# Two-layer gated block on one core: the argmax counts turned by DMA instead of TensorE, a new opening, pieces of 256, 512, 512, 512

## The reference, cut to what matters

```python
xn = layernorm(x)                                   # rows of 512, no scale or shift
w  = weight * (mask of 32x32 blocks is on)          # 512 x 512
s  = xn @ w.T + bias
inter = xn @ c1_w.T @ c2_w.T                        # rank 16, then 1792 columns
idx = argmax of inter in each of the 56 blocks of 32 columns
h   = relu(xn . w1[idx]);  g = silu(h @ w2t[idx])   # only the 56 chosen rows count
x   = x + s * g
```

## Time and profile before

| | us |
|---|---|
| median of 3 runs | 694.86 (693.66 to 695.56) |
| profiled execution, device time | 693.95 |
| its span, first to last instruction | 692.2 |
| mean granted TensorE clock | 0.993 |

### The profile page before, as it was taken

One profiled execution on the slowest core, in us unless ns is written; L12 is line 12 of the kernel. 1 busy time (PEld: TensorE's weight loads), 2 busy tenths in 40 slices (PEclk: granted clock), 3 DMA queues, 4 the chain that ended last, 5 costly groups with the idle time before them and its releaser, 6 DMA issues.

```text
span 692.2 us, 8636 instructions
## 1 busy us (share of the span) xinstructions
PE 659.1 (95%) x3078; PEld 518.1 (75%) x3078; DVE 457.0 (66%) x715; ACT 214.4 (31%) x379; POOL 231.7 (33%) x185
## 2 busy tenths in 40 slices
PE   2699999999999999999999999989999999999997
PEld 2577777877787777787777777657877877787787
DVE  7877775596665596665597776674856566485543
ACT  3424343312222412222312233443145125313610
POOL 1516455450000540000661226433514242341441
PEclk9899999999999999999999999999999999999999
DMA  8940000040000130000152110040031013002001
GB/s 235 386 166 1 0 1 0 32 152 1 0 1 0 47 136 0 0 0 0 45 207 80 58 62 0 32 153 0 31 110 43 1 45 136 0 30 91 2 16 46
DMA packets 19535, 40.66 MB, mean 59 GB/s; under 512 B 2032, under 2 KB 2416, under 8 KB 18864
## 3 DMA queue, kind: packets, MB, share of 16 engines
q1 hardware_dynamic: 19504, 40.25, 16.8%
HBM read 31.85 MB, written 8.39 MB: 58 GB/s over the span
## 4 chain that ended last, share of the span: by engine, by line
PE 84%; DVE 10%; issue 3%; DMA 1%; ACT 1%; POOL 0%; SPq 0%; DVEq 0%; ACTq 0%
PE bank L404 74%; PE bank L338 2%; PE bank L1141 2%; DVE eq L862 2%; PE bank L1236 2%; DVE seg_top L860 1%; PE bank L1104 1%; PE bank L1122 1%; DVE counts L872 1%; PE bank L1273 1%; DVE h_lo L896 1%; DVE ws_lo L925 1%; DMA x_tile<-in_x 1%; DVE x_tile L378 1%; DVE h L887 0%
## 5 line engine op out<-in xcount | busy, mean ns | idle before, releaser
L404 PE MATMUL bank<-w_hi_t,h_hi 128*128 128x512 f32 x224 | 93.7, 418 | 1.7 <-DVE h_lo L896 1.7
L698 ACT ACTIVATE h_hi<-h 128x512 fp32r<-128x512 f32 x56 | 35.4, 632 | 182.8 <-DVE h L887 182.8
L872 DVE TENSOR_TENSOR_SCAN counts<-restart,eq 128x512 bf16<-128x512 bf16 (+1 forms) x64 | 88.3, 1380 | 2.1
L404 PE MATMUL bank<-xT_hi,w_hi_t 128*128 128x512 f32 x224 | 88.9, 397 | 0.0
L404 PE MATMUL bank<-w_hi_t,h_lo 128*128 128x512 f32 x224 | 88.5, 395 | 0.0
L404 PE MATMUL bank<-w_lo_t,h_hi 128*128 128x512 f32 x224 | 88.5, 395 | 0.0
L404 PE MATMUL bank<-xT_hi,w_lo_t 128*128 128x512 f32 x224 | 88.5, 395 | 0.0
L404 PE MATMUL bank<-xT_lo,w_hi_t 128*128 128x512 f32 x224 | 88.4, 395 | 0.0
L860 DVE TENSOR_REDUCE seg_top<-bank 128x16 f32<-128x512 f32 (+1 forms) x64 | 39.5, 618 | 72.7 <-PE bank L1122 72.7
L384 POOL TENSOR_TENSOR g_tile<-g_tile,s_tile 128x512 f32<-128x512 f32 x31 | 40.6, 1311 | 95.2 <-DVE g_tile L909 56.4
L612 POOL TENSOR_TENSOR prod_lo<-prod,prod_hi 128x512 fp32r<-128x512 f32 x32 | 40.7, 1292 | 74.4 <-ACT prod_hi L736 74.4
(11 more groups left out here) (184 smaller groups left out, 1326.2 us busy)
## 6 DMA issues: line engine op xcount, KB each, us to landing
w_raw<-in_w SPq DMA_DIRECT2D x28, 256.0 KB, 10.1
x_res<-in_x SPq DMA_DIRECT2D x4, 1024.0 KB, 8.2
mid_state<-g_tile SPq DMA_DIRECT2D x16, 256.0 KB, 2.1
x_tile<-mid_state SPq DMA_DIRECT2D x4, 1024.0 KB, 7.6
x_res<-mid_state SPq DMA_DIRECT2D x4, 1024.0 KB, 5.6
out<-g_tile SPq DMA_DIRECT2D x15, 256.0 KB, 2.0
x_tile<-in_x SPq DMA_DIRECT2D x3, 1024.0 KB, 5.4
b_raw<-in_lora_b SPq DMA_DIRECT2D x2, 1024.0 KB, 4.9
```

The lines of the kernel that those rows point to most:

```text
L404: last = nc.tensor.matmul(dst, a, b, start=(start and n == 0), stop=(stop and n == len(mms) - 1))
L698: nc.scalar.activation(h_hi[:, it % 2, :], h[:], ACT.Copy).then_inc(h_hi_done, 1)
L872: nc.vector.tensor_tensor_scan(counts[:, p % 2, tt, 0:PW[p]], restart[:, 0:PW[p]], eq[:, 0:PW[p]], 0.0, ALU.mult, ALU.add).then_inc(sel_co ...
```

## The change

Seven things are changed together, nearly all in layer 0.

1. The counts are turned by DMA. `transpose_counts` is gone from TensorE. After the scan of a selection ScalarE issues one transposing DMA (`turn_counts`) from `counts` to `first`, which now lies in SBUF with two pieces' room; there are 16 for a chunk, of 128x512 or 128x256 bf16. VectorE's mask waits for the landing at the first tile of each piece. `counts` has one piece's room, and a scan waits for the landing of the turn of the piece before.
2. The pieces are 256, 512, 512, 512 wide instead of 512, 512, 512, 256. The selections of piece 0 and of row tiles 0 and 1 of piece 1 stand in the head, the other ten (`NEXT`) at it 0 to 9.
3. Selections use two banks in turn, `sels`; one waits for the equality of the last but one. `h` has two buffers, and relu runs one tile ahead.
4. The rank product of the next chunk moves from the head to the end of the body, between the parts of the last down product, and `t_rest` with it, ahead of the silu.
5. The opening: x comes in four row tiles, each normalized as it lands (`first_rows`); 14 matmuls of constants run first on TensorE; w1 tiles 0 and 1 are loaded ahead, mask and weight behind six others. The mask's block sums come at it 3 of chunk 0, the switch at 4, its products with the weight at 4 and 5, `ws_lo` at 6 and 7, and the s products ahead of up 9 and up 11. The body's first selections of chunk 0 (piece 1) come two per tile at it 0 and 1.
6. Epsilon is added by VectorE, so GpSimd has one instruction for the inverse root. Some constants move between VectorE and GpSimd.
7. In layer 0 GpSimd makes the four products of the gate first and then the four sums.

```diff
-    PW = [min(BANK, INTER - p * BANK) for p in range(PIECES)]
+    PW = [INTER - BANK * (PIECES - 1)] + [BANK] * (PIECES - 1)
+    PO = [sum(PW[:p]) for p in range(PIECES)]
+    AT = [(p, j) for p in range(PIECES) for j in range(PW[p] // P)]
+    NEXT = [(p, tt) for p in range(1, PIECES) for tt in range(S // P)][2:]
...
+        first = span_t.take("first", [P, 2, TT, S], BF16)
+        counts = span_t.take("counts", [P, TT, BANK], BF16)
...
-        h = span_t.take("h", [P, S])
...
+        h = span_t.take("h", [P, 2, S])
...
+        def first_rows(dve):
+
+            for tt in range(TT + 1):
+                if tt < TT:
+                    dve.wait_ge(ld_x if tt == TT - 1 else ld_x_first[tt], 16)
+                    nc.vector.bn_stats(bn[:, tt, :], x_tile[:, tt, :]).then_inc(stats_in, 1)
+                    dve.wait_ge(stats_in, tt + 1)
+                    nc.vector.bn_aggr(mean_var[:, tt, :], bn[:, tt, :]).then_inc(stats, 1)
+                    dve.wait_ge(stats, tt + 1)
+                    nc.vector.tensor_scalar(mean_var[:, tt, 1:2], mean_var[:, tt, 1:2], EPS, None, ALU.add)\
+                        .then_inc(var_eps, 1)
+                if tt:
+                    dve.wait_ge(rstd_done, tt)
+                    rows_scale(tt - 1)
...
-        sel = banks[6]
-        mask_bank = banks[5]
-        first = banks[7][:].bitcast(BF16)[:, 0:S]
+        sels = [banks[6], banks[7]]
+        warm_bank = banks[5]
...
+        WARM = 14
+        WS_AT = (5, 6)
+        MASK_N = TT * NEXT[WS_AT[0] - 1][0] + NEXT[WS_AT[0] - 1][1]
+        S_AT = (9, 11)
...
-            sp.dma_start(mask_nat[:], mask).then_inc(ld_mask, 16)
+            for tt in range(TT):
+                sp.dma_start(x_tile[:, tt, :], x_rows[0][:, tt, :]).then_inc(ld_x if tt == TT - 1 else ld_x_first[tt], 16)
+            sp.dma_start(c1_nat[:], c1_w).then_inc(ld_c1, 16)
+            for it in range(2):
...
+                    sp.dma_start(mask_nat[:], mask).then_inc(ld_mask, 16)
+                    sp.dma_start(ws_raw[:], w_s0).then_inc(ld_ws0, 16)
...
+            def turn_counts(c, p, tt):
+
+                act.wait_ge(sel_count, c * NSEL + p * TT + tt + 1)
+                if p >= 2:
+                    act.wait_ge(h_masked, c * IT + PO[p - 1] // P)
+                elif not (isinstance(c, int) and c == 0):
+                    act.wait_ge(h_masked, c * IT)
+                act.sem_inc(turns, 1)
+                act.dma_start_transpose(first[:, p % 2, 0:PW[p] // P, rows(tt)], counts[:, tt, 0:PW[p]])\
+                    .then_inc(ld_first[tt], 16)
+
             def head(c):
-                t_round(c)
-                for tt in range(TT):
+                for tt in range(2):
                     s_read(c, tt)
+                    turn_counts(c, 0, 2 * tt)
+                    turn_counts(c, 0, 2 * tt + 1)
+                for tt in range(2, TT):
+                    s_read(c, tt)
+                turn_counts(c, 1, 0)
+                turn_counts(c, 1, 1)
+                relu(c, 0)
+
...
+                if it in WS_AT:
+                    for k in range(2):
+                        k += 2 * (it - WS_AT[0])
+                        act.wait_ge(ws0_masked, k + 1)
+                        nc.scalar.activation(ws_hi[:, k, :], ws_raw[:, k, :], ACT.Copy).then_inc(ws_hi_done, 1)
+                if it + 2 in S_AT:
+                    for tt in range(2):
+                        s_read(0, 2 * S_AT.index(it + 2) + tt)
...
+                turned = c * PIECES + p
+                if not (isinstance(turned, int) and turned == 0):
+                    dve.wait_ge(ld_first[tt], turned * 16)
...
-                t_rest(c)
-                for tt in range(TT - 1):
+                for tt in range(TT):
                     select(c, 0, tt)
-
-            def body(c, last):
-                select(c, 0, TT - 1)
+                for tt in range(2):
+                    select(c, 1, tt)
+
+            def body(c, opening, last):
                 for it in range(IT):
-                    if 0 < it < 4 * (PIECES - 1):
-                        select(c, it // 4 + 1, it % 4)
+                    todo = [(1, 2 * it), (1, 2 * it + 1)] if opening and it < 2 else NEXT[it:it + 1]
                     dve.wait_ge(relu_done, c * IT + it + 1)
-                    dve.wait_ge(first_tr, c * IT + it + 1)
-                    nc.vector.scalar_tensor_tensor(h[:], first, 1.0, h[:], ALU.is_equal, ALU.mult).then_inc(h_masked, 1)
+                    p, j = AT[it]
+                    if j == 0:
+                        for tt in range(TT):
+                            dve.wait_ge(ld_first[tt], (c * PIECES + p + 1) * 16)
+                    nc.vector.scalar_tensor_tensor(h[:, it % 2, :], first[:, p % 2, j, :], 1.0, h[:, it % 2, :],
+                                                   ALU.is_equal, ALU.mult).then_inc(h_masked, 1)
+                    if it == IT - 1:
+                        for tt in range(2):
+                            rows_lo(dve, c + 1, tt)
                     if IT - 8 <= it < IT - 4:
                         rows_stats(dve, c + 1, it - (IT - 8))
...
+                    if opening and it == WS_AT[0] - 1:
+                        mask_switch()
+                    if todo:
+                        select_largest(c, *todo[0])
...
+                    if todo:
+                        select_count(c, *todo[0])
+                    if todo[1:]:
...
+                    if opening:
+                        if it == WS_AT[0] - 2:
+                            mask_counts()
+                        if it == WS_AT[0] - 1:
+                            mask_ws(range(0, 2))
+                        if it == WS_AT[0]:
+                            mask_ws(range(2, 4))
+                        if it in (WS_AT[0] + 1, WS_AT[0] + 2):
+                            ws_rest(range(2 * (it - WS_AT[0] - 1), 2 * (it - WS_AT[0] - 1) + 2))
+                for tt in range(2, TT):
                     rows_lo(dve, c + 1, tt)
+                if not last:
+                    t_rest(c + 1)
                 for tt in range(TT):
 
                     dve.wait_ge(tanh_done, c * TT + tt + 1)
...
+            def s_product(c, tt):
+
+                if isinstance(c, int) and c == 0:
+                    pe.wait_ge(ws_split, KD)
+                    pe.wait_ge(relu_done, S_AT[tt // 2] - 1 + tt % 2)
+                elif tt >= 2:
...
+                n = p * TT + tt
+                if n == 0:
                     pe.wait_ge(t_split, c + 1)
-                else:
-                    pe.wait_ge(sel_eq, c * NSEL + p * TT + tt)
-                nc.tensor.matmul(sel[:, 0:PW[p]], t_stack[:, rows(tt)],
...
-            def transpose_counts(c, it):
-
-                pe.wait_ge(sel_count, c * NSEL + (it // 4 + 1) * TT)
-                if it:
-                    pe.wait_ge(h_masked, c * IT + it)
-                for tt in range(TT):
-                    last = nc.tensor.transpose(first[:, rows(tt)], counts[:, it // 4 % 2, tt, rows(it % 4)], ident_bf[:])
-                last.then_inc(first_tr, 1)
...
-                rank_product()
+                select(c, 0, 0)
+                select(c, 0, 1)
                 s_product(c, 0)
+                select(c, 0, 2)
+                select(c, 0, 3)
                 s_product(c, 1)
-                select(c, 0, 0)
+                select(c, 1, 0)
+                select(c, 1, 1)
                 s_product(c, 2)
-                select(c, 0, 1)
                 s_product(c, 3)
-                select(c, 0, 2)
-
-            def body(c, first):
-                if not first:
...
+            def body(c, first, last):
+                for it in range(1, IT):
+                    if first and it in S_AT:
+                        s_product(0, 2 * S_AT.index(it))
+                        s_product(0, 2 * S_AT.index(it) + 1)
+                    if first and it - 1 in S_AT:
+                        pe.wait_ge(s0_read, 2 * S_AT.index(it - 1) + 2)
+                    elif first and it in S_AT:
+                        pe.wait_ge(s0_read, 2 * S_AT.index(it) + 1)
+                    up_product(c, it)
+                    if first:
+                        first_chunk(it)
+                    elif it <= len(NEXT):
+                        select(c, *NEXT[it - 1])
                     if it >= 2:
                         pe.wait_ge(h_split, c * IT + it - 1)
-                        if first and it == 2:
-                            pe.wait_ge(s0_read, TT)
                         down_product(it - 2, range(TT)).then_inc(down_done, 1)
+                        if first and it == 3:
+                            select(0, *NEXT[2])
+                pe.wait_ge(sel_eq, c * NSEL + NSEL)
+                for tt in range(2):
+                    transpose_rows(pe, c + 1, tt)
+                pe.wait_ge(relu_done, c * IT + IT - 1)
+                transpose_rows(pe, c + 1, 2)
                 pe.wait_ge(relu_done, c * IT + IT)
-                transpose_rows(pe, c + 1, 1)
```

(16 more changed lines are left out.)

371 lines of the change are left out of this document (193 added, 178 removed).

## The result

The changed kernel takes 719.84 us (median of 4 runs, 717.33 to 723.27) against 694.26 (4 runs, 692.24 to 695.56): ratio 1.037, 95% interval 1.0329 to 1.041. It is slower, as the largest of the three chances said, but far outside the range of 684 to 707. The profiled execution took 720.03, its span 718.2.

The account below looks back on a forecast made before the run. TensorE was taken to bound the kernel, VectorE the changed opening. Profiled 693.95 + 10.6 (chunk 0) - 5.8 (heads) - 3.5 (chunk 3) = 695.2, forecast 696 as median; range 684 to 707, own range 691 to 702.

Parts of the forecast that it names:

- the largest of the three chances: Whole kernel: slower, chance 0.44, against faster 0.39 and same 0.17.
- Chunk 0, forecast +10.6: Chunk 0 ends at about 139 instead of 128.4, 10.6 us lost; bounds 1.5 and 21 lost.
- Start: Opening: rank product starts at 13.5 instead of 16.41, 2.9 us saved; 1.6 more if the warmed clock is high.
- the fourth rival: Opening: warming does nothing, rank product at 0.43 again, all later by 1.6: 698 us; part of the forecast's range.
- L: Time from a scan's end to the landing of its turned counts: 3 us, bounds 2 and 5.
- The rival of late turns: From L = 4.5 each chunk waits at piece 1, chunk 0 three times; 710.5 us at L = 6.5; chance 0.21.
- VectorE's 54.4: Chunk 0, its 0 to 7: VectorE's own work from mask 0 at 28.4 to the last ws_lo, 54.4 us.
- Waits, forecast 6.0: Chunk 0, VectorE's waits: 3.0 and 1.5 for turns, 0.5 for the switch, 1 for a queued selection; sum 6.0.
- From the first s product to the end, forecast 51: Chunk 0 after ws_lo: 202 matmuls 47.1 us, row transposes 1.8, half clock 2.
- 88.8 rounded down to 88: Chunk 0, last ws_lo: 28.4 + 54.4 + 6.0 = 88.8, taken as 88 since not every scan meets POOL.
- Heads, forecast 1.9 saved: Chunks 1 to 3: period 100.2 instead of 102.1, 1.9 us saved each, 5.8 in all.
- Chunk 3, forecast 5.4 saved: Chunk 3: the period's 1.9 us saved, and 3.5 off its waits of 3.6 and the pauses beside them.

Follow-up runs that it names:

- e7_sels: Changed kernel with GpSimd's rstd earlier, loads held for two turns, TensorE's heads reordered, and chunk 0's selections issued ahead of products: 700.39 us, ratio 1.0125.
- e2_loads: Changed kernel with SyncE waiting for the four turns of piece 0 before the loads from w1 4 on: 719.85 us, ratio 1.0375.
- e5_pace: Changed kernel with SyncE holding loads twice, for the turns of piece 0 and of piece 1, mask and masked weight behind the second: 721.05 us, ratio 1.0411.
- e1_pool: Changed kernel with chunk 1's rstd put ahead of the last w2 rest and four bias sums on GpSimd: 711.26 us, ratio 1.0231.
- e12: Changed kernel with the masked weight at the front of chunk 0, GpSimd's rstd earlier and TensorE's heads reordered: 699.20 us, ratio 1.007.
- e13: Changed kernel with only the masked weight put back to the front of chunk 0: 714.02 us, ratio 1.0291.
- e3_fill: Changed kernel with twelve idle bf16 products filling TensorE's two waits ahead of s product 1 in heads of chunks 1 to 3: 714.02 us, ratio 1.0293.
- e15_all_rounds: e11_all with ScalarE rounding weights ahead of the turn in chunk 0's steps: 694.44 us, ratio 1.0003.
- e9_spread: e7_sels with later weight loads of chunk 0 each waiting for an up product, mask at step 5, next rows at step 7: 696.59 us, ratio 1.0039.
- e11_all: e9_spread with chunk 0's s products at up 10 and 12, and 16 more idle products ahead of the rank product: 690.88 us, ratio 0.9964.

## Why the prediction was wrong

**Chunk 0, forecast +10.6, measured +25.95.** By its own terms:
- Start. The rank product at 14.11 instead of 13.5, and at half clock: it ends 2.2 us later than forecast (17.58, not 15.4). The warming products ended at 7.69, the row transposes followed, and after 3.04 us of idle time the clock had fallen (0.61 from 14 to 18), as the fourth rival said. Luck has a part in it: in e7_sels, with the same opening, the rank product started at 12.58, after 1.96 us, and took 2.10.
- L, forecast 3 and taken as one number. It is 2.3 to 2.4 with no loads ahead and 7.24 behind loads. I had the row for that (10.1 for a load in the opening) and set it aside because the turns use another queue; e2_loads shows that the other queue does not keep them apart. With the start (1.3 of it), mask 0 came at 34.15 instead of 28.4: +5.8. The rival of late turns had such an L and 710.5 us, but for every turn; here it was piece 0 alone, and no run shows what this lateness costs by itself, since e2_loads and e5_pace only moved it. The Trainium skill (DMA: Bandwidth & Descriptors, Anatomy of one DMA) has a fixed cost and a rate, measured for DMAs that GpSimd issues, from which 128 KB would take an estimated 2.3; the trace agrees for ScalarE's turns with no loads ahead of them (2.42), and not for those behind loads.
- VectorE's 54.4. Measured 46 (mask 0 to the last ws_lo, 60.4, less 14.4 of waits): -8.4. I charged each scan 1.54; alone it takes 1.22, and only 1 of these 10 met GpSimd. The ten selections took 26.1 instead of 30.0, and the four products with the switch and the four ws_lo 4.8 instead of 8.0.
- Waits, forecast 6.0, measured 14.4: 7.5 for selections queued behind other products (3.78 and 2.78 behind 24 matmuls, and 0.89), 4.2 for turns, 2.7 for ScalarE and the mask's count. This is the step that failed most in method: I had counted one such queueing (1 us at step 1), priced at full clock, though I had forecast the half clock after TensorE's waits myself. e7_sels moved the first s product 3.5 us by issuing them earlier, the rest of what it gained there was its opening. That TensorE would idle for over 20 us in this stretch was right (22.0).
- From the first s product to the end, forecast 51, measured 59.7: 7.55 of it the wait behind GpSimd's order. I had put the change to the row norms at "nothing, TensorE covers both" and never walked GpSimd's list, in which the bias sums of the late s products now stood ahead of rstd. e1_pool left 2.30 of it and made this part 5.7 us shorter.

Together 5.8 - 8.4 + 8.4 + 8.7 + 0.8 (88.8 rounded down to 88) = 15.3. The errors have both signs: the 8.4 too much for VectorE's own work hid a third of the rest. With 4.7 in chunks 1 and 2, 5.2 in chunk 3 and -0.6 in layer 1 this makes up the 24.8 us between 695.2 and the 720.03 of the profiled execution, but for rounding.

That the masked weight comes last, "so TensorE has no s products" to run meanwhile, was the reason I gave. It is a part of it: with the masked weight first (e12, e13) TensorE's early waits shrink, and then the loop through ScalarE takes the time. The prediction had no term for ScalarE's issue of a turn in the bodies (it names only the head: "ACT's 6 issues in the head lie beside 16 us"); it is 1.2 us each, and, more, everything behind it in program order waits for the scan.

**Heads, forecast 1.9 saved, measured 0.4 lost.** The first two waits were right (0.70 and 2.19, forecast 2.8 to 3.5 together); the third, of about 1, did not come. The step that failed is the clock: no term for it in the heads, where the earlier trace rows had shown 0.50 behind 5.81 us. It costs 2.3 (s product 1 alone) to 2.5 a head (e3_fill); without it the period is 100.0, the forecast's 100.2. In part this is chance too: the same waits passed at the full clock in one head of e1_pool and one of e2_loads.

**Chunk 3, forecast 5.4 saved, measured 0.15.** 2.3 is the head's clock, of which e3_fill got 1.7 back. The waits did not go: 0.51, 1.61 and 2.52 against the earlier trace rows. VectorE is slowed there by GpSimd: h_lo took 3.60 at 407.22 beside a rest of 3.51 at 406.75. That the second buffer of h does not help where VectorE itself is late was only read from this, not tried.

**Two SBUF inputs beside GpSimd.** I gave the mask 0.15 us for reading `first` from SBUF. A mask that meets GpSimd takes 1.72 instead of 0.68, a scan 2.31 instead of 1.22. The Trainium skill (SBUF — State Buffer, Who interferes with whom) says that a VectorE instruction with two SBUF inputs contends with a GpSimd instruction that reads SBUF. The traces agree, with a price of 1.0 to 1.1 us a meeting.

Right were: rank product early, body step 5.82, layer 1 unchanged, the sign. What stays open: what the late landing of piece 0 costs by itself, what makes the roundings ahead of the turn cost 5.6 us in e15_all_rounds, and when a wait of 2 us brings the clock down.

## What to carry to other kernels

When work is reordered, walk the program order of every engine it touches, the idle ones too, and ask of each wait what is queued behind it: three of the misses here (GpSimd's rstd, TensorE's selections, ScalarE's turns) were instructions that stood in line behind something that had become late. A DMA's landing is a matter of what else is in flight (2.3 and 7.2 us here), and moving a burst of loads moved the lateness; spread them. A wait of TensorE can cost up to twice its length, since what follows may run at half clock (2.89 us of waits, 2.3 of clock here). And before a position in one trace is compared with one in another, compare a point that lies ahead of both edits: e7_sels owed 2.6 of its 6 us to its opening.

## What the runs showed of the hardware

- A 128x512 turn by DMA holds ScalarE's queue 1.2 us (1182 to 1532 ns, 64 of them) and lands 2.3 to 2.4 us after issue, up to 11.8 behind loads.
- Granted clock in the heads: 0.80 with waits of 0.70 and 2.19 us in all three of the changed kernel; 1.00 with the waits filled by idle bf16 products (0.23 left of each second one); but also 1.00 in e1_pool's second head with 0.69 and 2.18, unfilled, and in its first with 0.66 and 1.11.
- The rank product after an idle time of 1.96 us took 2.10 us in e7_sels, all at the full clock, and ran at 0.43 us a matmul in e1_pool.
- Ten runs of e9_spread lie between 691.5 and 699.3 us, but for one at 702.1; those of e11_all between 688.8 and 692.1, those of the kernel before between 691.2 and 695.5 (25 runs). Why e9_spread's differ more is not shown; the openings above are a part of what differs between executions.
